# Causal attention in two token halves, with the mean taken out by a matrix product and squares on ScalarE

## The reference

```python
x = x + _L1_conv_ref(_gn(x), ...)        # the result is called x2 in the kernel
t = _to_tokens(x)
t = t + _L2_attn_ref(_ln_t(t), Wq, Wk, Wv)

def _ln_t(v, eps=1e-05):
    m = jnp.mean(v, axis=-1, keepdims=True)
    s = jnp.var(v, axis=-1, keepdims=True)
    return (v - m) / jnp.sqrt(s + eps)

def _L2_attn_ref(query, Wq, Wk, Wv):
    q = jnp.einsum('btd,du->btu', query, Wq)
    k = jnp.einsum('btd,du->btu', query, Wk)
    v = jnp.einsum('btd,du->btu', query, Wv)
    scores = jnp.einsum('bqu,bku->bqk', q, k) / jnp.sqrt(T)
    scores = scores + NEG * (1.0 - causal)
    return jnp.einsum('bqk,bku->bqu', softmax(scores), v)
```

## Time and profile before

| | us |
|---|---|
| median of three executions | 215.9 |
| lowest and highest of them | 211.64 and 216.04 |
| the profiled execution | 212.2 |
| span of its instructions | 210.4 |
| TensorE busy | 180.1 |
| VectorE busy | 154.0 |
| ScalarE busy | 97.8 |
| GpSimd busy | 39.3 |

### The profile page before, as it was taken

One profiled execution on the slowest core, in us unless ns is written; L12 is line 12 of the kernel. 1 busy time (PEld: TensorE's weight loads), 2 busy tenths in 40 slices (PEclk: granted clock), 3 DMA queues, 4 the chain that ended last, 5 costly groups with the idle time before them and its releaser, 6 DMA issues.

```text
span 210.4 us, 6984 instructions
## 1 busy us (share of the span) xinstructions
PE 180.1 (86%) x3046; PEld 132.5 (63%) x3054; DVE 154.0 (73%) x347; ACT 97.8 (47%) x240; POOL 39.3 (19%) x57
## 2 busy tenths in 40 slices
PE   7799989998998999964898798598589969978994
PEld 2677669897897999621344684235236827646872
DVE  2789997989999999869777266596668757647201
ACT  2743998688787877611003260210768620016200
POOL 5970000021440440440100301233000000120000
PEclk9999999999999999999799999969965899999999
DMA  6930435555543520000142140000210081000000
GB/s 181 296 118 5 125 115 194 153 180 165 181 153 125 173 61 3 4 0 5 30 167 89 27 111 1 0 5 25 71 30 0 6 180 36 3 0 3 0 3 25
DMA packets 9203, 16.03 MB, mean 76 GB/s; under 512 B 2536, under 2 KB 3912, under 8 KB 9044
## 3 DMA queue, kind: packets, MB, share of 16 engines
q1 hardware_dynamic: 9028, 15.28, 24.0%
q10 hardware_dynamic: 144, 0.30, 0.4%
HBM read 15.15 MB, written 0.42 MB: 74 GB/s over the span
## 4 chain that ended last, share of the span: by engine, by line
PE 65%; DVE 17%; ACT 7%; issue 5%; POOL 2%; DMA 2%; POOLq 1%; DVEq 0%
PE ps L1550 63%; POOL rstd L583 2%; DMA cst<-in_cst 2%; ACT arena L646 1%; DVE att L1128 1%; DVE stu_fq L1453 1%; ACT onehot L845 1%; DVE arena L455 1%; ACT table L646 1%; ACT arena L866 1%; DVE onehot L1078 1%; ACT arena L730 1%; DVE arena L1534 1%; DVE arena L1058 1%; ACT onehot L787 1%
## 5 line engine op out<-in xcount | busy, mean ns | idle before, releaser
L1550 PE MATMUL ps<-table,onehot 128*128 128x64 bf16 x1728 | 52.6, 193 | 3.2 <-issue 1.9
L1550 PEld LDWEIGHTS ps<-table,onehot 128*128 128x128 bf16 x1728 | 51.3, 98 | 4.7 <-issue 4.2
L1550 PE MATMUL ps<-spare 128*128 128x512 bf16 x107 | 31.4, 423 | 9.3 <-DVE rexp L1369 2.3
L730 ACT ACTIVATE arena<-ps 128x512 f32<-128x512 f32 (+1 forms) x40 | 21.6, 552 | 12.5 <-PE ps L1550 12.3
L455 POOL TENSOR_TENSOR arena<-arena,w4p 128x288 f32<-128x288 f32 x21 | 16.2, 801 | 55.8 <-DVE arena L455 55.7
L1550 PEld LDWEIGHTS ps<-spare 128*128 128x128 bf16 x115 | 11.0, 108 | 23.4 <-issue 5.4
L583 POOL TENSOR_TENSOR rstd<-var_eps,cst 128x4 f32<-128x4 f32 (+2 forms) x9 | 8.8, 981 | 82.5 <-DVE var_eps L947 56.0
L1550 PE MATMUL ps<-arena 128*32 128x66 f32 (+6 forms) x388 | 22.1, 278 | 0.2 <-DVE arena L1330 0.2
L646 ACT ACTIVATE arena<-ps 128x512 f32<-128x512 f32 (+4 forms) x17 | 7.3, 465 | 31.2 <-PE ps L1550 25.5
L1550 PEld LDWEIGHTS ps<-arena 128*32 128x32 f32 (+3 forms) x388 | 18.3, 147 | 4.3 <-issue 1.6
L1078 DVE TENSOR_SCALAR onehot<-indexb,cst 128x2304 bf16<-128x2304 bf16 (+1 forms) x24 | 17.7, 772 | 0.0
(11 more groups left out here) (280 smaller groups left out, 307.3 us busy)
## 6 DMA issues: line engine op xcount, KB each, us to landing
indexb<-index_rows SPq DMA_DIRECT2D x20, 288.0 KB, 3.3
stu_fq<-index_rows SPq DMA_DIRECT2D x8, 288.0 KB, 3.4
arena<-in_toep SPq DMA_DIRECT2D x2, 514.0 KB, 5.9
l<-in_l SPq DMA_DIRECT2D x1, 646.5 KB
stu_fq<-in_stu SPq DMA_DIRECT2D x1, 560.0 KB, 3.7
onehot<-in_l3w SPq DMA_DIRECT2D x1, 512.0 KB
table<-stu_mixed SPq DMA_DIRECT2D x4, 128.0 KB, 2.4
l<-in_l SPq DMA_DIRECT2D x1, 384.0 KB, 6.7
```

Of the source, the lines that this page charges most:

```text
L730: nc.scalar.activation(gv[:, b % 2, :, at:at + count, :], ps[:, SB[n % len(SB)], 0:count * SLOT].rearrange("p (s a d) -> p a s d", s=count ...
L1550: return nc.tensor.matmul(out_ap, lhsT, rhs, start=start, stop=stop)
```

## The change

It does five things. (1) GpSimd builds, early in the kernel, a 128 x 128 matrix `centre` = I - J/32, where J is one within a block of 32 channels of one image; a product with it turns x2 and takes off the mean over channels at once. (2) TensorE makes the centred tokens of each half that way, half 0 in bank 0 and half 1 in bank 3; ScalarE squares them (`Square`), VectorE sums and scales, GpSimd's power and VectorE's multiplication go by halves. Plain tokens `x2t` are still made for the residual, now in bank 2, and copied behind the statistics. (3) The projections, their copies and the keys go by halves; the scores of the first tokens follow half 0, with maxima and exponentials of their own, and the mask and scores of the second tokens follow half 1 and wait for the exponential of the same bank. (4) The selection products move ahead of the wait for x2, and wpick and nwpick ahead of `kinv`. (5) Fillers in this stretch go from twelve to four.

```diff
@@ gpsimd
+            by_image = centre[:].rearrange("p (b c) -> p b c", b=B)
+            nc.gpsimd.tensor_scalar(by_image, rep(c["bmask"], C), -1.0 / C, None, ALU.mult).then_inc(g0.sem, g0.step("outer"))
+            pool_e.wait_ge(g0.sem, g0["outer"])
+            nc.gpsimd.tensor_tensor(out=centre[:], in0=centre[:], in1=ident, op=ALU.add).then_inc(g0.sem, g0.step("centre"))
...
-            pool_e.wait_ge(v3.sem, v3["eps"])
             pool_e.wait_ge(g0.sem, g0["rstd1"])
-            power(rstd[:], var_eps[:], c["neghalf"], "rstd2")
-            pool_e.wait_ge(g0.sem, g0["rstd2"])
+            for half in range(2):
+                cols = slice(half * T // 2, (half + 1) * T // 2)
+                pool_e.wait_ge(v3.sem, v3[f"eps{half}"])
+                power(rstd[:, cols], var_eps[:, cols], c["neghalf"][:, cols], f"rstd2{half}")
+            pool_e.wait_ge(g0.sem, g0["rstd21"])
@@ scalar
+            for h in range(NH):
+                act.wait_ge(t2.sem, t2[f"x2C{h}"])
+                nc.scalar.activation(half_of(lsq, h), centred_x2(h), ACT.Square).then_inc(a2.sem, a2.step(f"sq{h}"))
...
-            act.wait_ge(t3.sem, t3["lnT"])
-            copy(ln_ch, ps[:, 0, 0:N], a3, "lnT")
-            act.wait_ge(t3.sem, t3["qc"])
-            copy(qc, ps[:, 1, 0:N], a3, "qc", float(N) ** -0.5)
+            for h in range(NH):
+                act.wait_ge(t3.sem, t3[f"lnT{h}"])
+                copy(half_of(ln_ch, h), ps[:, 0, h * P:(h + 1) * P], a3, f"lnT{h}")
+                act.wait_ge(t3.sem, t3[f"qc{h}"])
+                copy(half_of(qc, h), ps[:, 1, h * P:(h + 1) * P], a3, f"qc{h}", float(N) ** -0.5)
             act.wait_ge(t3.sem, t3["vt"])
             copy(vt1[:, :, 0:C], tok(ps[:, 3, 0:N]), a3, "vt")
...
-            for b, h in ((b, h) for b in range(B) for h in range(NH)):
-                t = h * B + b
-                if h == 0:
-                    act.wait_ge(v3.sem, v3[f"second{b}"])
+            for t in range(T):
+                h, b = t // B, t % B
+                act.wait_ge(v3.sem, v3[f"{('first', 'second')[h]}{b}"])
@@ vector
+            for h in range(NH):
+                mean_square(v3, h, a2)
             dve.wait_ge(t2.sem, t2["x2T"])
-            nv.tensor_copy(x2t[:], ps[:, 5, 0:N]).then_inc(v2.sem, v2.step("x2t"))
-            dve.wait_ge(v2.sem, v2["x2t"])
-            layernorm(x2t[:], v3, "rstd2")
-            dve.wait_ge(t3.sem, t3["kc"])
-            nv.tensor_copy(kc, ps[:, 2, 0:N]).then_inc(v3.sem, v3.step("kc"))
+            nv.tensor_copy(x2t[:], ps[:, 2, 0:N]).then_inc(v2.sem, v2.step("x2t"))
+            for h in range(NH):
+                dve.wait_ge(g0.sem, g0[f"rstd2{h}"])
+                nv.tensor_tensor(out=tiles4(half_of(ln[:], h)), in0=tiles4(centred_x2(h)), in1=rep(half_of(rstd[:], h), C), op=ALU.mult)\
+                    .then_inc(v3.sem, v3.step(f"ln{h}"))
...
+            keys_copied(0)
+            largest_first(0)
+            largest_first(1)
+            keys_copied(1)
+            largest_first(2)
+            largest_first(3)
@@ tensor
-            occupied(2, 7)
+            weights_prepared("selection")
+            pe.wait_ge(g0.sem, g0["centre"])
             pe.wait_ge(v2.sem, v2["x2"])
             for h in range(NH):
-                ins = nc.tensor.transpose(ps[:, 5, h * P:(h + 1) * P], x2[:, h * P:(h + 1) * P], ident)
+                mm(centred_x2(h), x2[:, h * P:(h + 1) * P], centre[:]).then_inc(t2.sem, t2.step(f"x2C{h}"))
+            for h in range(NH):
+                ins = nc.tensor.transpose(ps[:, 2, h * P:(h + 1) * P], x2[:, h * P:(h + 1) * P], ident)
             ins.then_inc(t2.sem, t2.step("x2T"))
-            weights_prepared("selection")
...
-            occupied_after(v2, ("x2t", 3), bank=7)
...
-            occupied_after(v3, ("eps", 3), bank=0)
...
+            occupied_after(v3, ("eps1", 2), bank=1)
+            def projected(h):
+                cols = slice(h * P, (h + 1) * P)
+                pe.wait_ge(v3.sem, v3[f"ln{h}"])
+                nc.tensor.transpose(ps[:, 0, cols], ln[:, cols], ident).then_inc(t3.sem, t3.step(f"lnT{h}"))
+                if h == 0:
+                    pe.wait_ge(aw.sem, aw["taps"])
+                    masked(2)
+                pe.wait_ge(a3.sem, a3[f"lnT{h}"])
+                mm(ps[:, 1, cols], p2["wq"], ln_ch[:, cols]).then_inc(t3.sem, t3.step(f"qc{h}"))
+                mm(ps[:, 2, cols], p2["wk"], ln_ch[:, cols]).then_inc(t3.sem, t3.step(f"kc{h}"))
+                if h:
+                    for half in range(NH):
+                        cols = slice(half * P, (half + 1) * P)
+                        ins = mm(ps[:, 3, cols], ln_ch[:, cols], p2["wv"])
+                    ins.then_inc(t3.sem, t3.step("vt"))
+                pe.wait_ge(a3.sem, a3[f"qc{h}"])
+                pe.wait_ge(v3.sem, v3[f"kc{h}"])
+            projected(0)
+            for b in range(B):
+                rows = slice(b * C, (b + 1) * C)
+                mm(ps[:, 4 + b, 0:P], qc[rows, 0:P], kc[rows, 0:P], start=False).then_inc(t3.sem, t3.step(f"early{b}"))
+            projected(1)
+            for b in range(B):
+                rows = slice(b * C, (b + 1) * C)
+                pe.wait_ge(a3.sem, a3[f"exp{b}"])
+                masked(b, slice(2 * P, 3 * P))
                 mm(ps[:, 4 + b, P:2 * P], qc[rows, P:2 * P], kc[rows, 0:P], start=False, stop=False)
                 mm(ps[:, 4 + b, 2 * P:3 * P], qc[rows, P:2 * P], kc[rows, P:2 * P], start=False)\
                     .then_inc(t3.sem, t3.step(f"score{b}"))
-            occupied(4, 0)
+            occupied(2, 0)
```

More of the change, by code:

```diff
@@ L246, in hybrid @@
         fold2 = sb("fold2", [P, 2 * D])
+        centre = sb("centre", [P, P])
         late3 = table[:].bitcast(F32)
@@ L276, in hybrid @@
         g0 = Steps(sem("pool_steps"), "qkvpad qpad stackpad kvpad xpad rstd0 vdiag bnvar bninv sigma "
-                   + "foldz folda foldb"
-                   + " rstd1 rstd2 ones rstd30 rstd31 gated rstd40 rstd41 "
+                   + "foldz folda foldb outer centre"
+                   + " rstd1 rstd20 rstd21 ones rstd30 rstd31 gated rstd40 rstd41 "
                    "rstd50 rstd51")
@@ L318, in hybrid @@
         t1 = Steps(sem("tensor_corner_sums"), f"corners{L - 2}")
-        t2 = Steps(sem("tensor_conv"), "attT proj poolred katt conv x2T")
-        a2 = Steps(sem("scalar_conv"), "attT poolred kexp y1")
+        t2 = Steps(sem("tensor_conv"), "attT proj poolred katt conv x2C0 x2C1 x2T")
+        a2 = Steps(sem("scalar_conv"), "attT poolred kexp y1 sq0 sq1")
         v2 = Steps(sem("vector_conv"), "x1 stats moments eps xpad pool poolbd kmax kneg "
                    + " ".join(f"mix{k}_{i}" for i in range(3) for k in range(4)) + " kinv bmix bsum ksum binv bcent bscale bshift x2 ones x2t")
[L323 to L326, removed]
+        v3 = Steps(sem("vector_attn"), "var0 eps0 var1 eps1 ln0 ln1 kc0 first0 first1 kc1 first2 first3 "
+                   + " ".join(f"second{b}" for b in range(B)) + " pt0 pt1 pt3 sinv ctx x3")
+        a3 = Steps(sem("scalar_attn"), "lnT0 qc0 lnT1 qc1 vt " + " ".join(f"exp{t}" for t in range(T)) + " pt2")
+        t3 = Steps(sem("tensor_attn"), "lnT0 qc0 kc0 early0 early1 early2 early3 lnT1 qc1 kc1 vt score0 score1 score2 score3 pt0 pt1 pt2 pt3 pv")
         v4 = Steps(sem("vector_moe"), "sum0 cen0 sq0 var0 eps0 sum1 cen1 sq1 var1 eps1 ln0 ln1 "
@@ L476, in queries_of, with centred_x2 @@
             return ap.rearrange("p (g h b n) -> p g h b n", g=HG, h=NH, b=B)[:, i // B * 2:i // B * 2 + 2, :, i % B, :]
+        def centred_x2(h):
+            return ps[:, 3 * h, 0:P]
         def taps_product(b):
@@ L907, in _ @@
             nv = nc.vector
[L909 to L924, removed]
             def less_mean(src, v, q):
@@ L941, in squares, with mean_square @@
                 nv.tensor_tensor(out=half_of(lsq, q), in0=cen, in1=cen, op=ALU.mult).then_inc(v.sem, v.step(f"sq{q}"))
-            def mean_square(v, q):
-                dve.wait_ge(v.sem, v[f"sq{q}"])
+            def mean_square(v, q, squared=None):
+                squared = squared or v
+                dve.wait_ge(squared.sem, squared[f"sq{q}"])
                 nv.reduce_sum(half_of(lvar[:], q), tiles4(half_of(lsq, q)), axis=AX.X).then_inc(v.sem, v.step(f"var{q}"))
@@ L1296, in _ @@
                                                 op0=ALU.mult, op1=ALU.add).then_inc(v2.sem, v2.step(f"mix{k}_{i}"))
+            dve.wait_ge(vz.sem, vz["wcol"])
+            nv.tensor_scalar(wpick[:].rearrange("p (r e) -> p r e", r=4),
+                             c["fold"].unsqueeze(1).broadcast_to([P, 4, C]), wcol[:], None, ALU.mult)\
+                .then_inc(vz.sem, vz.step("wpick"))
+            dve.wait_ge(vz.sem, vz["wpick"])
+            nv.tensor_scalar(nwpick[:], wpick[:], -1.0, None, ALU.mult).then_inc(vz.sem, vz.step("nwpick"))
             nv.reciprocal(kinv[:], ksum_[:]).then_inc(v2.sem, v2.step("kinv"))
@@ L1347, in _ @@
             dve.wait_ge(v3.sem, v3["ctx"])
```

(19 more changed lines are left out.)

13 lines of the change are left out of this document (6 added, 7 removed).

## The result

The changed kernel is slower: 217.75 us (median of four, 217.09 to 218.26) against 214.69 for the kernel before, ratio 1.024 with an interval of 1.015 to 1.034. In a second group of runs it took 217.79 us against 212.88, ratio 1.032 (1.024 to 1.040). (Each ratio compares only the faster executions of either kernel, so it need not equal the quotient of the medians.) Its profiled execution took 217.09 us with a span of 215.3; before, 212.2 and 210.4. The range on record ended at 217.2.

The account below looks back on a forecast made before the run. No engine is full: the changed stage is one thread hopping between engines, 14.9 of 210.4 us. Terms of -2.4, +0.1 and +1.75 gave 0.55 us earlier, 215.35 from the median 215.9 (likeliest 215.3), range 210.6 to 217.2.

Parts of the forecast that it names:

- Part 1: Edits ahead of x2: wpick moved earlier makes y1 about 0.1 us late, x2 ready at 113.10; selection products fill a hole.
- Part 2: Normalisation: half 0 normalised 2.68 us after x2, at 115.78 instead of 118.18, a lead of 2.4 us; half 1 at 116.84.
- rival 4: Square on ScalarE reloads activation tables, two loads, +1.7 us after partial cover, 217.0 us in sum; chance 0.05.
- Part 3: Projections and first scores: halves in series on TensorE's queue spend the lead; exp0 runs 120.32 to 120.69, TensorE idles 0.7 us.
- Part 4: Second scores to third image's transposes: 0.50 us per image on TensorE, four images 2.0; transposes at 123.83, plus 0.1 wait.
- Rival 2: TensorE's clock falls in the attention with fewer fillers and new waits: 217.0 us for a 3.4 us low stretch; chance 0.12.
- the longer low clock: TensorE's clock low for 10.5 us in the attention: +5.2 us, 220.6 us; left out of the range.
- Rival 1: More of the normalisation lead survives the attention, up to the whole 2.4 us: 213.5 us; chance 0.15.
- rival 3: The low-clock stretch at 154.3 to 164.8 falls otherwise; the kernel sits on the lower level, 211.1 us; chance 0.13.

## Why the prediction was wrong

The 6.25 us of the stage divide as follows, each term from two profiled executions: the normalisation -1.36 (13.56 for 14.92), the attention in halves +1.54 (15.10 for 13.56), masks between the scores +1.69 (16.79 for 15.10), the low clock +4.38 (21.17 for 16.79). The terms hold for this order of steps. The one of the halves contains more than the second pass: the second masks, which before lay beside other work, the two turns that are left, and the 0.54 us for which the transposes wait.

**Part 1, edits ahead of x2: the number right, partly by luck.** The selection went into the hole, and TensorE started on x2 at 113.10, as forecast. But y1 wasn't late: it started at 111.93, 0.05 sooner than before. The 0.1 arose behind x2, which TensorE took up 0.11 us after it was written (0.02 before). Upstream differences between executions are larger than this term.

**Part 2, normalisation: right.** Half 0 was due 2.68 us behind x2 and came 2.77 behind the centring product's start (115.58 + 0.29); half 1 was due at 116.84 and came at 116.85. Square ran 128x128 in 0.277, the lower of the two bounds, and no second table load stood before it, so rival 4 is out. The lead of half 0 over the earlier trace rows is 2.3 us. That of half 1 is 1.33, and only that one is kept when the attention runs in one piece.

**Part 3, first scores: right, to 0.1 us.** exp0 was forecast at 120.32 behind the value copy and started at 120.42; TensorE idled 0.82 ahead of the second mask (forecast 0.7); the second pair of first maxima stood behind the copy of kc1.

**Part 4, second scores: the step that failed.** "2 x 0.11 + 4 x 0.07 = 0.50" took the price of a mask record from a run of masks and the price of a score record from a run of scores. In the change they alternate, and an image costs 1.06 at full clock. Four images: 2.2 us missing, of which 1.7 comes back when the masks are batched. The text had one part of this as a bound, "if the 16 second-score records cost 0.11 instead of 0.07 it is +0.65": they did cost 0.11. For the other part, eight turns of 0.19, 1.5 us, it had no term. With 1.06 for 0.50 the sum of the text becomes -0.55 + 2.24 = +1.69, and the stage with its clock kept has +1.87: the rest of the sum was sound to 0.2 us.

**Rival 2 happened.** It had the place, and its price was right: for a low stretch of 10.5 us it gave +5.2, and 10.2 us cost 4.38. It had 0.12. The step that failed is the reason against it: the row at 129 to 132 us shows 1.86 of 3.00 us busy at full clock, but it is a stretch of 3 us, and the new waits are spread over 7, from 114 to 121. Why the clock fell stays open (see the end); that the waits have to do with it is what the fillers show. The text put the longer low clock outside the range while its only long low stretch elsewhere lasted 10.5 us, a length that the trace itself offered.

**Rival 1 didn't happen, and rival 3 can't explain it.** The low stretch at 154.3 to 164.8 is still there, moved to about 159.4 to 169.6. The mean clock over the execution hardly moved, 0.959 to 0.952. Before, two of the three low stretches lay mostly on fillers, and only the one at 154.3 on products that set the end; afterwards both low stretches lie on such products. Nor are there two levels 4.3 us apart, which the text read out of three executions: the 25 of the kernel before in the first group lie from 209.89 to 215.82 us with no gap over 0.8.

## What to carry to other kernels

Price an instruction in the company that it will have: where small products on a few rows alternate with products on all rows, count each record at the step that it has alone (0.11 us here) and not at an average over records that overlap (0.07), and add what the trace shows for a turn (0.19). Or batch each kind. When a pass is cut in two to start earlier, count the waits that the cut gives TensorE, over the whole stretch and not the longest one. A lead that two halves in series spend again may be worth keeping alone: here the cheaper normalisation without the halves was the only part that shortened the stage.

## What the runs showed that was not expected

- The cost of the alternation: 1.06 us for a mask of two records and four score records at full clock, 0.42 for six records on the image's 32 rows. At half clock the same alternation took 1.87. The scores of four images, put together, overlap to 0.68 us for all sixteen records.
- What decides the fall of the clock stays open. It stayed in one kernel after 5.21 us busy of 7.00, and in another after 5.13 it fell 3.7 us later; it stayed with the fillers of before cut to four. With eight added to the changed kernel, six of ten executions had the mean clock of the one in which it is seen to stay. No kernel was tried that moves the waits without changing their number.
- The start of the stage, x2, lay between 112.69 and 115.62 us in kernels that have nearly the same program ahead of it. In the stretch from 100 to 105 us the clock was at 1.00 in those at 112.69 to 113.67, and between 0.50 and 0.69 in the ones at 113.84 to 115.62; only the profile of before, 0.70 with x2 at 113.05, stands out. This may make some of the 5 us and more by which executions of one kernel differ.
